# The third mixture layer of a four-layer kernel: from all experts for all tokens to eleven tiles of slots, each for one expert

## The reference, cut to what matters

```python
router_logits = xf @ Wr + br                       # xf: 2048 x 128, layer-normed h
topk_logits, topk_idx = jax.lax.top_k(router_logits, 1)
topk_gates = jax.nn.softmax(topk_logits, axis=1)   # one entry, so it is 1
for e in range(8):
    h = jax.nn.relu(xf @ W1[e] + b1[e])            # 2048 x 512
    oe = h @ W2[e] + b2[e]                         # 2048 x 128
    out = out + jnp.where((topk_idx[:, 0] == e)[:, None], topk_gates * oe, 0.0)
```

## Time and profile before

| what | us |
|---|---|
| median of 3 runs | 3297.83 |
| the profiled execution's own time | 3300.3 |
| its span, first to last instruction | 3298.5 |
| layer m2, from its first instruction to that of the next layer | 2624.70 to 2856.19 |
| of it: norm, routing, opening | 2624.70 to 2665.13 |
| of it: the 128 steps | 2665.13 to 2851 |

### The profile page before, as it was taken

One profiled execution on the slowest core, in us unless ns is written; L12 is line 12 of the kernel. 1 busy time (PEld: TensorE's weight loads), 2 busy tenths in 40 slices (PEclk: granted clock), 3 DMA queues, 4 the chain that ended last, 5 costly groups with the idle time before them and its releaser, 6 DMA issues. The chain is left out here.

```text
span 3298.5 us, 29241 instructions
## 1 busy us (share of the span) xinstructions
PE 2573.4 (78%) x8955; PEld 1522.9 (46%) x8955; DVE 2360.9 (72%) x3401; ACT 1333.6 (40%) x2106; POOL 1386.7 (42%) x841
## 2 busy tenths in 40 slices
PE   1887877687787754999578978399997589768499
PEld 0333333332332322666346646377775467523365
DVE  5699798669979975555566575578886668669556
ACT  2644544264454421222243433167774257410222
POOL 1499699449969951111114334100001210024266
PEclk9899899889989886999789989599998789879799
DMA  4244155125505502556100000121210021000021
GB/s 135 41 122 109 20 130 108 29 41 122 109 20 129 109 21 56 138 137 150 33 17 10 16 0 4 36 76 60 76 57 13 3 89 52 17 13 13 11 81 64
DMA packets 86601, 203.32 MB, mean 62 GB/s; under 512 B 12816, under 2 KB 25184, under 8 KB 77920
## 3 DMA queue, kind: packets, MB, share of 16 engines
q1 hardware_dynamic: 85952, 200.63, 24.0%
q0 software_dynamic: 512, 1.05, 0.1%
HBM read 198.76 MB, written 2.88 MB: 61 GB/s over the span
## 5 line engine op out<-in xcount | busy, mean ns | idle before, releaser
L532 DVE TENSOR_TENSOR m1x_HS<-m1x_R,m1x_HS 128x512 fp32r<-128x512 f32 x256 | 175.8, 691 | 69.2 <-ACT m1x_HS L500 64.8
L493 ACT ACTIVATE m1x_R<-m1x_ph,m1s_W 128x512 f32<-128x512 f32 x256 | 176.3, 689 | 107.1 <-PE m1x_ph L308 106.3
L1337 POOL TENSOR_TENSOR t2x_KM<-t2x_KT,t2x_HM 128x2048 f32<-128x2048 f32 x8 | 28.8, 3603 | 434.8 <-ACT t2x_KT L1410 416.6
L1677 POOL TENSOR_TENSOR t3xs_QH<-t3xs_HS,t3xa_Q 128x1536 f32<-128x1536 f32 x16 | 62.0, 3877 | 352.6 <-DVE t3xs_HS L1663 352.6
L829 DVE TENSOR_TENSOR m0x_T<-m0x_S,m0x_pb 128x512 f32<-128x512 f32 x128 | 88.1, 689 | 128.3 <-PE m0x_pb L308 120.8
L2080 PE MATMUL t0x1fs_acc<-t0x1fs_HC,g_ident 128*128 128x512 f32 x256 | 134.1, 656 | 38.2 <-POOL t0x1fs_HC L2161 38.1
L2080 PE MATMUL t0x0fs_acc<-t0x0fs_HC,g_ident 128*128 128x512 f32 x256 | 135.0, 660 | 36.4 <-POOL t0x0fs_HC L2161 36.3
L815 ACT ACTIVATE m0x_S<-m0x_pa 128x512 f32<-128x512 f32 x128 | 76.6, 598 | 213.1 <-PE m0x_pa L308 213.1
L2080 PE MATMUL t0x1bs_acc<-t0x1bs_HC,g_ident 128*128 128x512 f32 x256 | 130.8, 641 | 37.1 <-POOL t0x1bs_HC L2161 37.0
L2080 PE MATMUL t0x0bs_acc<-t0x0bs_HC,g_ident 128*128 128x512 f32 x256 | 130.4, 640 | 35.8 <-POOL t0x0bs_HC L2161 35.7
L2161 POOL TENSOR_TENSOR t0x1bs_HC<-t0x1bs_HS,t0x1bs_CB 128x1024 f32<-128x1024 f32 x64 | 149.2, 2360 | 13.2 <-PE t0x1bs_acc L2080 6.6
(11 more groups left out here) (908 smaller groups left out, 7652.2 us busy)
## 6 DMA issues: line engine op xcount, KB each, us to landing
m0x_GS<-m_gate_rows SPq DMA_DIRECT2D x64, 512.0 KB, 6.6
t0x0fs_CB<-t0x0f_bc_rows SPq DMA_DIRECT2D x32, 512.0 KB, 6.1
t0x0bs_CB<-t0x0b_bc_rows SPq DMA_DIRECT2D x32, 512.0 KB, 6.4
t0x1fs_CB<-t0x1f_bc_rows SPq DMA_DIRECT2D x32, 512.0 KB, 6.3
t0x1bs_CB<-t0x1b_bc_rows SPq DMA_DIRECT2D x32, 512.0 KB, 6.8
m1x_GS<-m_gate_rows SPq DMA_DIRECT2D x16, 1024.0 KB, 4.7
m1s_W<-in_L_w SPq DMA_DIRECT2D x16, 514.0 KB, 3.3
m2x_GS<-m_gate_rows SPq DMA_DIRECT2D x8, 1024.0 KB, 4.7
```

The source lines that it names most:

```text
L493: a.activation(R[:, s % 4, :], ph[s % 4][:, :], ACT.Relu, bias=W[:, e % RAW, weights.cut + c:weights.cut + c + 1]).then_inc(relu_ready, 1)
L532: v.tensor_tensor(HS[:, s % 4, 1, :], R[:, s % 4, :], HS[:, s % 4, 0, :].bitcast(F32), ALU.subtract).then_inc(low_made, 1)
L1337: nc.gpsimd.tensor_tensor(KM[:, i % 2, :, :], keys, spread(HM[:, :], W), ALU.mult).then_inc(km_made, 1)
L1677: nc.gpsimd.tensor_tensor(QH[:, j % 2, 0:SPLIT], HS[:, j % 2, 0:SPLIT], Q[:, 0:SPLIT], ALU.mult).then_inc(qh_pool, 1)
```

## The change

The layer m2 is no longer written by `relu_layer` but by two new functions; m1 keeps the old ones. The computation is the same.

**Routing (`route_sparse`).** Logits, top value and place are made as before. The choice of each token then becomes a slot number: two matmuls count the tokens ahead, DVE adds up the 16 tiles, gives each expert as many tiles of 512 slots as it needs (8 experts and 2048 tokens never need more than 11), and works out for each of the 11 tiles which expert it has. POOL fetches the weights of the first three tiles by row number (128 rows of 4116 bytes each) and puts the normed tokens into their slots in DRAM, 16 indirect transfers of 128 rows of 512 bytes. The slots were filled with zeros by SP before. The gate is 1 for each token, and is computed.

**Experts (`sparse_experts`).** 11 tiles of 4 steps, 44 in all. For each tile SP loads the 512 slot rows, PE turns them (4 transposes), ACT and DVE split them, ACT rounds the tile's weights and POOL makes their rest. Products, relu and split of the hidden value stay as they were, and so does the lead of three steps. There is no gate row: ACT reads the output with its bias (`read`), PE turns it back (`turn_out`), DVE copies it and SP stores the 512 rows. The waits inside: `turn_in(j)` waits for the tile's slot rows (`x_loaded`), `round_x(j)` for `turn_in(j)`, `round_w(j)` for the weights (`w_loaded`) and for the last product of tile j - 2, `second(s)` for DVE's part of the hidden value (`low_made`), `read(j)` for the last product of tile j and gives `y_read`, `turn_out(j)` waits for `y_read`, `copy_y(j)` for `turn_out(j)` and gives `yt_read`. Behind the last tile POOL fetches each token's row by its slot number, again 16 indirect transfers, and DVE adds it to `H`.

```diff
+def route_sparse(nc, name, XT, XN, ident, iota, earlier, pick, w_router, b_router, w12, E, out):
...
+            def _(sp):
+                sp.dma_start(wr[:, :], w_router[:, :]).then_inc(loaded, 16)
+                sp.dma_start(br[:, :], b_router.partition_broadcast(P)).then_inc(loaded, 16)
+                sp.wait_ge(blanked, 1)
+                for q in range(GROUPS):
+                    part = slot_rows[q * P * NT:(q + 1) * P * NT, :].rearrange("(p a) d -> p (a d)", a=NT)
+                    sp.dma_start(part, blank[:, :]).then_inc(cleared, 16)
...
+                pe.matmul(flat(before), earlier[:, 0, :], chosen16[:, :], start=True, stop=True)
+                pe.matmul(flat(inall), earlier[:, 1, :], chosen16[:, :], start=True, stop=True).then_inc(counted, 1)
...
+                dve.wait_ge(counted, 1)
+                link(v.memset(ahead[:, 0, :], 0.0))
+                for t in range(1, TILES):
+                    link(v.tensor_tensor(ahead[:, t, :], ahead[:, t - 1, :], inall[:, t - 1, :], ALU.add))
+                link(v.tensor_tensor(count[:, :], ahead[:, TILES - 1, :], inall[:, TILES - 1, :], ALU.add))
+                link(v.tensor_tensor(over[:, :, :], spread(count[:, :], PER),
+                                     bounds[:, :].unsqueeze(1).broadcast_to([P, E, PER]), ALU.is_gt))
+                link(v.tensor_reduce(used[:, :], over[:, :, :], AX.X, ALU.add))
+                link(v.tensor_tensor_scan(ends[:, :], ones[:, :], used[:, :], 0.0, ALU.mult, ALU.add))
...
+                v.tensor_copy(weight_row[:, :], expert[:, :]).then_inc(weight_row_ready, 1)
...
+                v.tensor_copy(slot[:, :], place[:, :]).then_inc(slot_ready, 1)
...
+            def _(pool):
+                nc.gpsimd.memset(blank[:, :], 0.0).then_inc(blanked, 1)
+                pool.wait_ge(weight_row_ready, 1)
+                for j in range(len(w_loaded)):
+                    pool.indirect_dma_start(W[:, j, :], None, w12,
+                                            bass.IndirectOffsetOnAxis(ap=weight_row[:, j:j + 1], axis=0)).then_inc(w_loaded[j], 16)
+                pool.wait_ge(slot_ready, 1)
+                pool.wait_ge(cleared, 16 * GROUPS)
+                for t in range(TILES):
+                    pool.indirect_dma_start(slot_rows, bass.IndirectOffsetOnAxis(ap=slot[:, t:t + 1], axis=0),
+                                            XN[:, t, :], None).then_inc(scattered, 16)
+
+def sparse_experts(nc, name, H, ident, w12, out_rows, r):
+    C, LAG = 4, 3
+    STEPS = NT * C
+    RAW = len(w_loaded)
...
+            def _(sp):
+                sp.wait_ge(scattered, 16 * TILES)
+                for j in range(3):
+                    sp.dma_start(XG[:, j, :, :], rows(slot_rows, j)).then_inc(x_loaded[j], 16)
+                for j in range(NT):
+                    sp.wait_ge(yt_read, j + 1)
+                    sp.dma_start(rows(out_rows, j), YT[:, j % 2, :, :]).then_inc(y_stored[j % 2], 16)
+                    if j + 3 < NT:
+                        sp.wait_ge(x_turned, j + 1)
+                        sp.dma_start(XG[:, j % 3, :, :], rows(slot_rows, j + 3)).then_inc(x_loaded[j % 3], 16)
...
+            def _(pool):
+                for j in range(NT):
+                    pool.wait_ge(w_high, j + 1)
+                    nc.gpsimd.tensor_tensor(WR[:, j % 2, 1, :], W[:, j % RAW, 0:CUT], WR[:, j % 2, 0, :].bitcast(F32),
+                                            ALU.subtract).then_inc(w_split, 1)
+                    n = j + RAW - 1
+                    if RAW <= n < NT:
+                        pool.wait_ge(w_split, n - RAW + 1)
+                        pool.wait_ge(y_read, n - RAW + 1)
+                        pool.indirect_dma_start(W[:, n % RAW, :], None, w12,
+                                                bass.IndirectOffsetOnAxis(ap=r["weight_row"][:, n:n + 1],
+                                                                          axis=0)).then_inc(w_loaded[n % RAW], 16)
+                for b in range(2):
+                    pool.wait_ge(y_stored[b], 16 * ((NT + 1 - b) // 2))
+                for t in range(TILES):
+                    pool.indirect_dma_start(YG[:, t, :], None, out_rows,
+                                            bass.IndirectOffsetOnAxis(ap=r["slot"][:, t:t + 1],
+                                                                      axis=0)).then_inc(gathered[t // GT], 16)
...
+            def _(pe):
...
+                def first(s):
+                    j, c = s // C, s % C
+                    if c == 0:
+                        pe.wait_ge(w_split, j + 1)
+                        pe.wait_ge(x_split, j + 1)
...
+                for s in range(STEPS):
+                    j, c = s // C, s % C
+                    if c == 0 and j + 1 < NT:
+                        turn_in(j + 1)
+                    if s + LAG < STEPS:
+                        first(s + LAG)
+                    second(s)
+                    if c == 1 and j:
+                        turn_out(j - 1)
+                turn_out(NT - 1)
...
+            def _(act):
...
+                for s in range(STEPS + 1):
+                    j, c = s // C, s % C
+                    if s < STEPS:
+                        relu(s)
+                    if s and (s - 1) % 2 == 0:
+                        high(s - 1)
+                    if s < STEPS and c == 0 and j + 1 < NT:
+                        round_w(j + 1)
+                        round_x(j + 1)
+                    if c == 3 and j:
+                        read(j - 1)
+                read(NT - 1)
...
+            def _(dve):
...
+                for s in range(STEPS):
+                    j, c = s // C, s % C
+                    low(s)
+                    if c == 0 and j + 1 < NT:
+                        split_x(j + 1)
+                    if c == 3 and j:
+                        copy_y(j - 1)
+                copy_y(NT - 1)
+                for t in range(TILES):
+                    if t % GT == 0:
+                        dve.wait_ge(gathered[t // GT], 16 * GT)
+                    v.scalar_tensor_tensor(H[:, t, :], YG[:, t, :], r["gate"][:, t:t + 1], H[:, t, :], ALU.mult, ALU.add)
...
-        relu_layer("m2", 8, 1, "L2_ffn_Wr", "L2_ffn_br", "L2_w12", "L2_ffn_b2")
+            route_sparse(nc, "m2r", XT, XN, ident, iota, consts["earlier"], consts["pick"], ins["L2_ffn_Wr"],
+                         ins["L2_ffn_br"], ins["L2_w12"], E, r)
+            sparse_experts(nc, "m2x", H, ident, ins["L2_w12"], out_rows, r)
```

More of the change, by code:

```diff
@@ L2865, in build @@
         recycle(nc)
-        relu_layer("m2", 8, 1, "L2_ffn_Wr", "L2_ffn_br", "L2_w12", "L2_ffn_b2")
+        with Stage(nc, "m2s") as s:
+            NT, E = 11, 8
+            XN = s.sb("XN", [P, TILES, P])
+            normalise(nc, "m2n", H, XT, ident, XN)
+            r = dict(tiles=NT, gate=s.sb("gate", [P, TILES]), slot=s.sb("slot", [P, TILES], U32),
+                     weight_row=s.sb("weight_row", [P, NT], U32), W=s.sb("W", [P, 3, ins["L2_w12"].shape[-1]]),
+                     w_loaded=[s.sem(f"w_loaded{j}") for j in range(3)], scattered=s.sem("scattered"),
+                     slot_rows=nc.dram_tensor("m2_slot_rows", (NT * GROUP, P), F32, kind="Internal").ap())
+            out_rows = nc.dram_tensor("m2_out_rows", (NT * GROUP, P), F32, kind="Internal").ap()
+            route_sparse(nc, "m2r", XT, XN, ident, iota, consts["earlier"], consts["pick"], ins["L2_ffn_Wr"],
+                         ins["L2_ffn_br"], ins["L2_w12"], E, r)
+            sparse_experts(nc, "m2x", H, ident, ins["L2_w12"], out_rows, r)
         recycle(nc)
@@ L2895, in lay_out @@
     d = {"x": a["x"]}
-    for n in ("L1_ffn_router_w", "L1_ffn_router_b", "L1_ffn_b2", "L2_ffn_Wr", "L2_ffn_br", "L2_ffn_b2"):
+    for n in ("L1_ffn_router_w", "L1_ffn_router_b", "L1_ffn_b2", "L2_ffn_Wr", "L2_ffn_br"):
         d[n] = a[n]
@@ L2902, in lay_out @@
                                         b1.reshape(E, 4, P).transpose(0, 2, 1)], axis=2)
+    d["L2_w12"] = np.concatenate([d["L2_w12"], a["L2_ffn_b2"][:, :, None]], axis=2).reshape(8 * P, -1)
     d["L0_tok_W"], d["L0_tok_b"] = a["L0_tok_W"], a["L0_tok_b"]
@@ L2912, in lay_out @@
     d["c_pick"] = np.concatenate([blocks % 8 == np.arange(8), blocks // 8 == np.arange(TILES), blocks * P,
-                                  np.zeros((P, TILES - 1))], axis=1).astype(np.float32)
+                                  blocks, np.zeros((P, TILES - 2))], axis=1).astype(np.float32)
     m = {n: a["L0_attn_" + n] for n in ("in_proj_w", "conv_w", "conv_b", "xproj_w", "dtproj_w", "dtproj_b", "A_log",
```

217 lines of the change are left out of this document (added).

## The result

The change makes the kernel slower: 3314.53 us (median of 13 runs, 3308.47 to 3317.15) against 3294.43 us of the kernel before (13 runs, 3281.82 to 3304.19) on the same chip. The ratio is 1.0061, 95% interval 1.0049 to 1.0073. The forecast was 3318 us, slower.

The account below looks back on a forecast made before the run. PE bounded the layer before; afterwards feeding the tiles would: first product at 2686.9 us, tiles, store, fetches and border summed to 2876.7 against 2856.19, 20.5 later, so 3297.83 + 20.5 = 3318 us, range 3304 to 3332 (8 in 10: 3285 to 3345).

Parts of the forecast that it names:

- its ring: Tile loop: y's read, POOL's weight transfer and split, products, turning, copy, store, slot-row load, next turning; 16.8 us at low clock.
- the sum: Stretches of layer m2 added from first product at 2686.9 us to the layer's end at 2876.7, 20.5 us later than before.
- The lead-in: Ahead of the first product: linked routing adds, weight transfers, 16 scatters, slot-row load and turning; first product 21.8 us later.
- One tile in the steady state: Tiles 1 to 8, from one turn_in to the next: 16.8 us at the low clock, 15.0 at full clock.
- an upper end of 18.1: Steady tile: PE's own stream behind POOL's split if its clock never came back, 18.1 us.
- The wait on POOL: Tile loop, rival: POOL's wait does not decide, slot rows bound a tile at 10.4 us; 51 us less, 3267 us; 15%.
- The clock: Tile loop, rival: PE's clock holds at 1.00, 15.0 us a tile, 14.4 us less, 3304 us; 12%.
- The dearer weight transfers: POOL's 11 weight transfers, rival: twice the 0.94 us gives 3328 us, cost by the bytes gives 3391; 15%.
- Behind the steps: After the last tile: store landing 2.8 us, 16 fetches and adds 22.5, layer border 0.97.
- The zero fill: Lead-in: SP's zeroing of the slots, 2.9 MB, would end as POOL reaches the scatter; costed at nothing.
- The other rule: Scatter and last store: by the skill's DRAM receipt rule each some 1.4 us later, 2.8 in all.

Follow-up runs that it names:

- e1: Against the changed kernel: POOL's split of a tile's weights put ahead of the weight transfer that waits for a read; 3276.73 us, ratio to before 0.9957.
- e9: e6 with POOL's order of the changed kernel put back, the weight transfer ahead of the next tile's split; 3282.30 us, ratio to before 0.9955.
- e2: Against the changed kernel: SP's load of slot rows put ahead of the output store and its wait; 3314.26 us, ratio to before 1.0068.
- e4: Against the changed kernel: 14 unused matmuls per tile added in PE's gap, tiles 1 to 8; 3309.84 us, ratio to before 1.0056.
- e3: The edits of e1 and e2 together, against the changed kernel; 3273.92 us, ratio to before 0.9949.
- e7: e6 with three raw weight buffers again instead of four; 3265.20 us, ratio to before 0.9903.
- e5: Against the changed kernel: only the first 4 of 16 scatters and of 16 fetches issued; 3284.27 us, ratio to before 0.9973.
- e6: e3 with four raw weight buffers for three, three split ones for two, rows turned two steps earlier (the dense version); 3233.60 us, ratio to before 0.9820.
- after: The changed kernel itself, against the kernel before; 3314.53 us, ratio to before 1.0061.

## Why the prediction was right

It came out near for its own reasons, the main one shown by e1 and e9. But one link of its ring was wrong, and its smaller errors cancel, which is luck: against the sum, the stretch up to tile 0 is 0.1 us shorter, tile 0 0.4 shorter (8.31), the eight tiles 1.0 shorter (133.42), the last two tiles up to the last store 1.6 longer (17.91 for 16.3), and the wait for that store 0.5 shorter. By its steps:

**The lead-in (first product 21.8 us later): right.** Measured from the layer's start, 62.38 us against 40.43, 21.95 later. Inside it the linked steps of DVE were cheaper: 15 adds of 8 columns took 2.91 us, 0.195 each for the 0.21 taken; the first weight transfer starts 0.8 us earlier than the sum had the rows. The scatters cost 1.277 us of pitch where the fetches of the earlier trace rows cost 1.26, and from the last scatter's issue to the load of its rows, with the border between, it is 3.30 us and not 2.5.

**One tile in the steady state (16.8): right, 16.68; the tile shown is 17.08.** Term by term in that tile, forecast and measured: `turn_in` to the end of y's read 5.3 and 4.96; from there to the split's end 3.6 and 4.28; product 1.44 and 1.45; second 1.28 and 1.28; turning to the copy 1.2 and 1.10; copy and store issue 1.1 and 1.08; load 2.9 and 2.88. Three terms are off. ACT's instructions start 0.5 to 0.6 us apart where I added their durations (0.62 and 0.69), which makes the read come 0.7 sooner. `round_w`, which the sum had done before the tile begins, stands on ACT at its start, and `round_x` begins 1.03 us into the tile where the sum had 0.64. And between the end of the read and POOL's transfer lie 0.83 us that I had at nothing.

**What closes the tile's ring: the wrong link.** The load of the slot rows stood in the sum as the link that closes the ring. e2 takes its wait out and the tile gives up only 0.4 us: `round_w`, with its wait for PE's last product, closes a ring of the same length. The prediction took the high part that `round_w` makes as ready at about 0, and had of this ring only PE's own stream, as an upper end of 18.1. In the tile shown `turn_in` is done at 2711.32, and `round_x` starts at 2711.69 because `round_w` holds ACT until then, so the load's wait is hidden in this tile. That the number is right all the same is luck: at the end of this tile the two links are 0.04 us apart.

**The wait on POOL (rival, 15%): excluded.** e1 moves only the split out from behind it and gains 35 us of layer; e9 brings it back into a kernel with all else loosened and loses 48. The rival's tile of 10.4 is where e1's would be at full clock, by the estimate above.

**The clock (rival, 12%): it falls, as forecast.** Behind POOL's gap the granted clock is 0.50 to 2726 and back at 1.00 from 2727; e4 prices it at 1.5 us a tile, where the forecast had 1.8. What the sum left out is the clock in tile 9: there 4 us of its work run at a mean of 0.62, which is most of the 1.6 us that the end is longer (an estimate). The rule of the Trainium skill that the prediction weighed ("TensorE: Matmul & The Clock Gate", section "HAM oscillation — how this bites in real kernels": bursts parted by waits lose the clock at each tile) agrees with this trace: 0.71 over the eight tiles. In e3 one tile of eight kept 1.00 over a wait.

**The dearer weight transfers (rival, 15%): excluded.** POOL is held 0.94 to 1.12 us by a transfer of 128 rows of 4116 bytes, against 0.94 for rows of 512 bytes. (In e3 and e7 such transfers held POOL for up to 1.46 us.)

**Behind the steps (22.5 us of fetches, the store 2.8): right.** From the first fetch to the next layer, 23.39 us for 22.5 and the border's 0.97. The fetches start 2.3 us after the last tile's store is issued, where I had 2.8. e5 shows that both series are paid in full. The zero fill, costed at nothing, is off the path: the scatters follow the weight transfers at the same 0.30 us of gap.

The other rule that was weighed, in the Trainium skill's "DMA: Bandwidth & Descriptors", section "Anatomy of one DMA — SWDGE (gpsimd) path", puts most of a transfer's fixed time into the receipt of the target, DRAM being the slowest; by it the scatter and the store would each have landed 1.4 us later than in the sum. The trace doesn't show that: the stores into DRAM land in 2.0 us and the scatters into it in 2.2, sooner than the sum had them (2.8 and 2.53), and sooner than the loads (2.8) and the fetches (2.5) out of it. The measurement decides. The section is about transfers that GpSimd issues, which the scatter is and SP's store is not. And the 2.6 us that the prediction took from the earlier trace rows as a store's is the row of a load (the trace of the kernel before has a store of that size at 2.6 too, which isn't shown).

**The median.** The time was 3.5 us below the forecast because the kernel before, over 13 runs, has a median 3.4 us below that of the three runs shown; the difference of the two kernels, 20.1 us, was forecast as 20.5.

## What to carry to other kernels

Removing two thirds of the bound engine's products gave nothing here while the queue that feeds it worked in order and held a wait: put what the bound engine needs next ahead of any instruction that waits for a later result, and give the waiting one more buffers. When several rings (split buffers, raw buffers, the turning of rows) have nearly the same length, loosening the next one gives little until all are loosened: e1 gained 35 us of layer, e2 2.5, both together 39, and e6 81, of which any one of three parts taken back costs 28 to 48. A loop that leaves the bound engine idle can pay twice, by the wait and by the clock behind it: price the work behind each wait at both levels. In series, indirect transfers of 128 rows followed each other on POOL every 1.24 to 1.35 us, with rows of 512 and of 4116 bytes alike, so count the transfers, not the bytes, and count those in series ahead of and behind the loop in full.

## What was unexpected of the hardware

- In the loop an indirect transfer starts 0.77 to 0.83 us after the end of the read that releases it (after: 2715.62 to 2716.45; e9: 2731.60 to 2732.37), though POOL is idle; in the lead-in the first one starts 0.28 us after the cast that releases it. Why isn't settled; no run here isolates it.
- The clock fell at a short gap and held over a longer one. In e1 PE's products end at 2736.22, the next starts at 2738.11, and the granted clock is 0.50 from 2737 on; in e3 PE stands for 3.14 us up to 2747.23 and the clock stays at 1.00. The runs give no rule for it.
- In the dense version the same transfers land later than in after: 256 KB of slot rows 4.0 us for 2.8, a store of 256 KB 3.9 for 2.0, weights 5.2 for 4.4:

```profile
m2x_XG<-m_slot_rows SPq DMA_DIRECT2D x11, 256.0 KB, 4.0
m_out_rows<-m2x_YT SPq DMA_DIRECT2D x11, 256.0 KB, 3.9
...
m2s_W<-in_L_w,m2s_weight_row POOLq DMA_INDIRECT x11, 5.2
```

(DMA issues of e6.) With 130 GB/s in its steps where after had 63, durations of a loose schedule are not those of a tight one.
